# Attention scores from halves of TensorE's rows, joined on three engines

## What is computed

```python
q = apply_rope(q, pos)
k = apply_rope(k, curr_seq_pos + jnp.arange(sk))
scores = jnp.einsum('bhqd,bhkd->bhqk', q, k) / scale
attn = jax.nn.softmax(scores + m[:, None, :, :], axis=-1)
```

## Time and profile before, and how to read it

| | us |
|---|---|
| median of 3 runs | 1569.04 (1567.05 to 1571.4) |
| profiled execution, its own time | 1573.28 |
| its span in the profile | 1571.5 |
| mean granted clock of TensorE | 0.979 of full speed |

### The profile page before, as it was taken

The page is one execution under the profiler, slowest core; times in us unless marked ns, Lnnn a source line. Parts: engine busy times, 40 slices in busy tenths (PEclk is TensorE's granted clock), DMA queues, the critical chain, the costliest instruction groups (busy, mean ns, idle before and its releaser), DMA issues. The chain is left out here.

```text
span 1571.5 us, 26176 instructions
## 1 busy us (share of the span) xinstructions
PE 1491.5 (95%) x8720; PEld 1313.4 (84%) x8720; DVE 1034.3 (66%) x2375; ACT 614.2 (39%) x1183; POOL 722.5 (46%) x586
## 2 busy tenths in 40 slices
PE   6889999999999999999999579999999999949998
PEld 5778888888888888888888479999999999938886
DVE  5737888878888778887788735455455455475552
ACT  5732222322223222222222246555555555455442
POOL 5734445554555545555455334333333333224554
PEclk9989999999999999999999789999999999969999
DMA  7830222212222122221221696343973343152221
GB/s 265 279 108 27 69 74 68 67 53 74 73 67 67 47 80 73 67 67 47 80 67 40 187 345 239 107 127 113 400 274 99 98 127 121 60 207 81 101 74 67
DMA packets 90991, 184.02 MB, mean 117 GB/s; under 512 B 8976, under 2 KB 34064, under 8 KB 90768
## 3 DMA queue, kind: packets, MB, share of 16 engines
q1 hardware_dynamic: 86848, 178.95, 35.5%
q10 hardware_dynamic: 4080, 4.26, 0.8%
HBM read 129.70 MB, written 53.48 MB: 117 GB/s over the span
## 5 line engine op out<-in xcount | busy, mean ns | idle before, releaser
L51 PE MATMUL q_ps<-x_hi,w_hi 128*128 128x512 f32 x1024 | 399.7, 390 | 3.4 <-PEq L66 3.4
L53 PE MATMUL q_ps<-x_hi,w_lo 128*128 128x512 f32 x1024 | 401.2, 392 | 0.0
L52 PE MATMUL q_ps<-x_lo,w_hi 128*128 128x512 f32 x1024 | 400.5, 391 | 0.0
L913 DVE TENSOR_TENSOR vw_lo<-vw_ps,vw_hi 64x256 fp32r<-64x256 f32 x512 | 215.9, 422 | 225.5 <-ACT vw_hi L873 220.4
L902 POOL TENSOR_TENSOR w_lo<-w_raw,w_hi 128x512 fp32r<-128x512 f32 x128 | 166.7, 1303 | 289.0 <-ACT w_hi L865 289.0
L838 PE MATMUL acc_ps<-vw_hi,x_hi 128*128 128x256 f32 x1024 | 290.3, 283 | 1.4 <-ACT vw_hi L873 1.4
L840 PE MATMUL acc_ps<-vw_hi,x_lo 128*128 128x256 f32 x1024 | 290.2, 283 | 0.0
L839 PE MATMUL acc_ps<-vw_lo,x_hi 128*128 128x256 f32 x1024 | 290.2, 283 | 0.0
L873 ACT CAST vw_hi<-vw_ps 64x256 fp32r<-64x256 f32 x512 | 187.5, 366 | 170.3 <-PE vw_ps L53 165.5
L595 POOL TENSOR_TENSOR q_lo<-rot,q_hi 128x512 fp32r<-128x512 f32 x128 | 165.0, 1294 | 190.3 <-ACT q_hi L561 190.2
L51 PEld LDWEIGHTS q_ps<-x_hi,w_hi 128*128 128x128 f32 x1024 | 192.9, 188 | 44.9 <-issue 3.6
(11 more groups left out here) (132 smaller groups left out, 2455.9 us busy)
## 6 DMA issues: line engine op xcount, KB each, us to landing
w_raw<-in_wo SPq DMA_DIRECT2D x128, 256.0 KB, 2.7
w_raw<-in_wq SPq DMA_DIRECT2D x32, 512.0 KB, 5.2
probs_scratch<-pt_hi SPq DMA_DIRECT2D x64, 256.0 KB, 2.6
probs_scratch<-pt_lo SPq DMA_DIRECT2D x64, 256.0 KB, 3.2
x_hi<-probs_scratch SPq DMA_DIRECT2D x32, 512.0 KB, 7.7
x_lo<-probs_scratch SPq DMA_DIRECT2D x32, 512.0 KB, 9.4
x_in<-in_x SPq DMA_DIRECT2D x16, 512.0 KB, 4.8
ahead_y<-in_x SPq DMA_DIRECT2D x8, 1024.0 KB, 6.5
```

The costliest lines, as they stand in the source:

```text
L51: pe.matmul(out, hi, rhs_hi, start=first, stop=False, **kw)
L52: pe.matmul(out, hi, rhs_lo, start=False, stop=False, **kw)
L53: return pe.matmul(out, lo, rhs_hi, start=False, stop=last, **kw)
L913: done = nc.vector.tensor_tensor(vw_lo[at], vw_ps[i][b * SK:(b + 1) * SK, h, :], vw_hi[at].bitcast(F32), ALU.subtract)
```

## The change

`key_hi` and `key_lo` become one tile `key_parts`. In each head's 64 rows it holds the high keys in the head's own 64 columns and the low keys in the other 64. Its zeroing on VectorE goes. The scores of a step are made as products of 64 rows by 128 columns: for each `c`, for `q_hi` and then `q_lo`, one for each head, into a PSUM tile of its own (`st_ps[0]`, `st_ps[1]`). A head's tile then holds its high-key sums in the head's own partitions and its low-key sums in the other 64; the product of low by low is now in the sums, too. ScalarE copies the low sums of both heads into the head's own partitions of `low_scores` (at the head of its slot), GpSimd adds the mask to that tile (at the head of its slot), and VectorE adds the high sums in two operations of 64 partitions, in place of the mask's addition. `rope_ps` goes, to make room in PSUM; the rotation multiplies by the cosine in place in `q_ps`, in another order, and TensorE waits for `rot_ready` before it fills these tiles again.

```diff
--- before.py
+++ after.py
@@ -365,8 +365,7 @@
             return ctx.enter_context(nc.semaphore(name))
 
         key_raw = sb("key_raw", [P, 2, B, SK])
-        key_hi = sb("key_hi", [P, 2, B, P], F32R)
-        key_lo = sb("key_lo", [P, 2, B, P], F32R)
+        key_parts = sb("key_parts", [P, 2, B, P], F32R)
         cos_q = sb("cos_q", [P, S])
         sin_q = sb("sin_q", [P, S])
         mask = sb("mask", [P, B, S])
@@ -374,6 +373,7 @@
         rot = sb("rot", [P, 2, S])
         q_hi = sb("q_hi", [P, 2, S], F32R)
         q_lo = sb("q_lo", [P, 2, S], F32R)
+        low_scores = sb("low_scores", [P, S])
         masked = sb("masked", [P, S])
         shifted = sb("shifted", [P, NBLK, BLK])
         probs = sb("probs", [P, NBLK, BLK])
@@ -386,16 +386,16 @@
         pt_hi = sb("pt_hi", [P, 2, S], F32R)
         pt_lo = sb("pt_lo", [P, 2, S], F32R)
         q_ps = [ps(f"q_ps{i}", [P, S]) for i in range(4)]
-        st_ps = ps("st_ps", [P, S])
+        st_ps = [ps(f"st_ps{h}", [P, S]) for h in range(2)]
         s_ps = ps("s_ps", [P, NBLK, BLK])
-        rope_ps = ps("rope_ps", [P, S])
         part_ps = ps("part_ps", [P, 2, NBLK])
 
         consts_in = sem("att_consts_in")
         w_in = [sem(f"w_in{c}") for c in range(2)]
         w_hi_ready = sem("w_hi_ready")
         w_lo_ready = sem("w_lo_ready")
-        key_zeroed = sem("key_zeroed")
+        st_low_ready = sem("st_low_ready")
+        low_masked_ready = sem("low_masked_ready")
         key_in = sem("key_in")
         key_hi_ready = sem("key_hi_ready")
         key_lo_ready = sem("key_lo_ready")
@@ -418,9 +418,17 @@
 
         block = ctx.enter_context(nc.Block())
 
-        def own_block(part, h):
-
-            return part[h * HALF:(h + 1) * HALF, :, :, h * SK:(h + 1) * SK]
+        def own_rows(h):
+
+            return slice(h * HALF, (h + 1) * HALF)
+
+        def high_keys(h):
+
+            return key_parts[own_rows(h), :, :, h * SK:(h + 1) * SK]
+
+        def low_keys(h):
+
+            return key_parts[own_rows(h), :, :, (1 - h) * SK:(2 - h) * SK]
 
         def raw_keys(h):
 
@@ -504,7 +512,7 @@
                     wait(pe, w_hi_ready, 2 * (hp - 1) + c + 1)
                     wait(pe, w_lo_ready, 2 * (hp - 1) + c + 1)
                 if c == 0 and ks[0] == 0:
-                    wait(pe, prod_ready, 2 * u - 2)
+                    wait(pe, rot_ready, 2 * u - 2)
                 for k in ks:
                     at = (slice(None), k, slice(b * S, (b + 1) * S))
                     last = three(pe, q_ps[2 * (j % 2) + c][:], w_hi[:, c, k, :], w_lo[:, c, k, :], x_hi[at], x_lo[at],
@@ -526,9 +534,12 @@
                     for c in range(2):
                         pe.wait_ge(q_hi_ready, 2 * u - 1 + c)
                         pe.wait_ge(q_lo_ready, 2 * u - 1 + c)
-                        last = three(pe, st_ps[:], key_hi[:, c, b, :], key_lo[:, c, b, :], q_hi[:, c, :], q_lo[:, c, :],
-                                     c == 0, c == 1)
-                    last.then_inc(st_done, 1)
+                        for n, part in enumerate((q_hi, q_lo)):
+                            for h in range(2):
+                                last = pe.matmul(st_ps[h][:], key_parts[own_rows(h), c, b, :], part[own_rows(h), c, :],
+                                                 start=c == 0 and n == 0, stop=c == 1 and n == 1)
+                                if c == 1 and n == 1:
+                                    last.then_inc(st_done, 1)
                 if has(g, j, 0):
                     queries(g, j, 1, range(KT // 2, KT))
 
@@ -545,19 +556,22 @@
             def slot(g, j, last):
                 u = STEPS_G * g + j
                 hp = 2 * g + j // B
+                if has(g, j, 2):
+                    for h in range(2):
+                        act.wait_ge(st_done, 2 * (u - 2) + h + 1)
+                        wait(act, masked_ready, u - 2)
+                        nc.scalar.copy(low_scores[own_rows(h)], st_ps[h][own_rows(1 - h)]).then_inc(st_low_ready, 1)
                 if j % B == 0 and has(g, j, 0) and not (isinstance(g, int) and g == 0 and j == 0):
                     split_w(hp, 1)
                 if j == 1:
                     act.wait_ge(key_in, 64 * (g + 1))
-                    if isinstance(g, int) and g == 0:
-                        act.wait_ge(key_zeroed, 1)
-                    wait(act, st_done, u - 1)
+                    wait(act, st_done, 2 * (u - 1))
                     for h in range(2):
-                        nc.scalar.copy(own_block(key_hi, h), raw_keys(h)).then_inc(key_hi_ready, 1)
+                        nc.scalar.copy(high_keys(h), raw_keys(h)).then_inc(key_hi_ready, 1)
                 if has(g, j, 1):
                     for c in range(2):
                         act.wait_ge(rot_ready, 2 * u - 1 + c)
-                        wait(act, st_done, u - 1)
+                        wait(act, st_done, 2 * (u - 1))
                         nc.scalar.copy(q_hi[:, c], rot[:, c]).then_inc(q_hi_ready, 1)
                 if j % B == B - 1 and not (last and j >= B):
                     split_w(hp + 1, 0)
@@ -581,12 +595,15 @@
             def slot(g, j, last):
                 u = STEPS_G * g + j
                 hp = 2 * g + j // B
+                if has(g, j, 2):
+                    pool.wait_ge(st_low_ready, 2 * (u - 2) + 2)
+                    nc.gpsimd.tensor_tensor(low_scores[:], low_scores[:], mask[:, (j - 2) % B], ALU.add).then_inc(low_masked_ready, 1)
                 if j % B == 0 and has(g, j, 0) and not (isinstance(g, int) and g == 0 and j == 0):
                     split_w(hp, 1)
                 if j == 1:
                     for h in range(2):
                         pool.wait_ge(key_hi_ready, 2 * g + h + 1)
-                        nc.gpsimd.tensor_tensor(own_block(key_lo, h), raw_keys(h), own_block(key_hi, h).bitcast(F32),
+                        nc.gpsimd.tensor_tensor(low_keys(h), raw_keys(h), high_keys(h).bitcast(F32),
                                                 ALU.subtract).then_inc(key_lo_ready, 1)
                         pool.wait_ge(key_lo_ready, 2 * g + h + 1)
                 if has(g, j, 1):
@@ -623,21 +640,22 @@
                 if has(g, j, 1):
                     q1, q2 = q_ps[2 * ((j - 1) % 2)][:], q_ps[2 * ((j - 1) % 2) + 1][:]
                     dve.wait_ge(q_done, 2 * u)
-                    nc.vector.tensor_tensor(rope_ps[:], q1, cos_q[:], ALU.mult)
-                    nc.vector.tensor_tensor(prod[:, 0], q2, sin_q[:], ALU.mult).then_inc(prod_ready, 1)
+                    nc.vector.tensor_tensor(prod[:, 0], q2, sin_q[:], ALU.mult)
                     nc.vector.tensor_tensor(prod[:, 1], q1, sin_q[:], ALU.mult)
+                    nc.vector.tensor_tensor(q1, q1, cos_q[:], ALU.mult).then_inc(prod_ready, 1)
+                    nc.vector.tensor_tensor(q2, q2, cos_q[:], ALU.mult).then_inc(prod_ready, 1)
                     dve.wait_ge(prod_ready, 2 * u - 1)
                     wait(dve, q_lo_ready, 2 * u - 3)
-                    nc.vector.tensor_tensor(rot[:, 0], rope_ps[:], prod[:, 0], ALU.subtract).then_inc(rot_ready, 1)
-                    dve.wait_ge(rot_ready, 2 * u - 1)
-                    nc.vector.tensor_tensor(rope_ps[:], q2, cos_q[:], ALU.mult).then_inc(prod_ready, 1)
+                    nc.vector.tensor_tensor(rot[:, 0], q1, prod[:, 0], ALU.subtract).then_inc(rot_ready, 1)
                     dve.wait_ge(prod_ready, 2 * u)
                     wait(dve, q_lo_ready, 2 * u - 2)
-                    nc.vector.tensor_tensor(rot[:, 1], rope_ps[:], prod[:, 1], ALU.add).then_inc(rot_ready, 1)
+                    nc.vector.tensor_tensor(rot[:, 1], q2, prod[:, 1], ALU.add).then_inc(rot_ready, 1)
                 if has(g, j, 2):
-                    b = (j - 2) % B
-                    dve.wait_ge(st_done, u - 1)
-                    nc.vector.tensor_tensor(masked[:], st_ps[:], mask[:, b], ALU.add).then_inc(masked_ready, 1)
+                    dve.wait_ge(low_masked_ready, u - 1)
+                    for h in range(2):
+                        dve.wait_ge(st_done, 2 * (u - 2) + h + 1)
+                        done = nc.vector.tensor_tensor(masked[own_rows(h)], st_ps[h][own_rows(h)], low_scores[own_rows(h)], ALU.add)
+                    done.then_inc(masked_ready, 1)
                     dve.wait_ge(masked_ready, u - 1)
                     nc.vector.transpose(s_ps[:].rearrange("p n k -> p (n k)"), masked[:]).then_inc(softmax_step, 1)
                     dve.wait_ge(softmax_step, SOFTMAX_STEPS * (u - 2) + 1)
@@ -667,9 +685,6 @@
                     wait(dve, probs_ready, u - 2)
                     nc.vector.reciprocal(row_inv[:], row_sum[:]).then_inc(inv_ready, 1)
 
-            for part in (key_hi, key_lo):
-                done = nc.vector.memset(part[:].bitcast(F32), 0.0)
-            done.then_inc(key_zeroed, 1)
             dve.wait_ge(consts_in, 48)
             over_key_heads(dve, slot, False)
 
```

## The result

The changed kernel takes 1568.11 us (median of 20 runs, 1565.79 to 1571.46), the kernel before, beside it, 1571.61 (20 runs, 1567.05 to 1575.32): a ratio of 0.9983 [0.9975, 0.9991]. The medians differ by 3.5 us, the means by 2.7, which is what the ratio says. A second set of runs gave 0.999 [0.9979, 1.0001], whose interval includes 1. The forecast was +1.0 us. The profiled execution took 1567.43 us, with a span of 1565.6.

What follows compares the result with a forecast made beforehand. TensorE's matmuls were taken to bound the kernel. The profiled 1573.3 us, +3.6 (tail) and -2.6 (steps), gives 1574.3; as the median lies 4.2 below that execution, the forecast was 1570.0 us, range 1543 to 1580.

Steps and rivals of the forecast that it cites:

- Streaming: TensorE's scores: eight half-row matmuls run as four side-by-side pairs of 0.23, 0.92 us instead of 1.38 per step.
- Rival (c): TensorE's scores: the row halves don't run side by side, +0.87 us per step, 1628 us; chance 0.08.
- Changing shape: TensorE around each score block: going to half rows and back costs 0.41 us, plus 0.01 for late second halves.
- 0.04 gained, **2.6 us** over 64 steps: TensorE's scores per step: 1.34 us instead of 1.38, streaming and shape change together.
- (a): TensorE's score block: no price for changing shape, 1543 us, chance 0.14; half the price, 1557 us, chance 0.12.
- (b): TensorE's score block: eight weight loads for six make it slower, 1577 us (chance 0.18) or 1591 us (chance 0.06).
- 1591: Inside the score block a half's next weights wait for its own matmul: 0.33 us per step, 21 us; chance 0.06.
- 1577: The two halves' first weight loads follow one another: 0.11 us more per step, 7 us; chance 0.18.
- VectorE, ScalarE, GpSimd hidden: Attention steps: joins of 0.68 each, copies of 0.60 each and an addition of 1.29 us stay behind TensorE's work.
- The two waits of TensorE: Attention stage of the kernel before: TensorE waits for the others twice, 5.1 and 4.7 us long.
- Tail: End of the attention stage, without cover: the last transposition starts at 898.2 instead of 894.60, 3.6 us later.
- The sum: Whole kernel: +3.6 in the tail less 2.6 in the steps, +1.0 us, the profiled execution at 1574.3.

Runs made afterwards that it cites:

- rotation_alone: The kernel before with only the changed rotation (cosine products in place, new order, TensorE waiting for the rotation's end), scores as before; 1568.64 us, ratio 0.9998.
- tail_early: The changed kernel with the last step's low copies and mask addition issued a slot earlier; 1566.52 us, ratio 0.9978.
- full_shared: Changed kernel with scores over all 128 rows, turning copies and tail work moved earlier, first head's sine product moved from VectorE to GpSimd; 1545.41 us, ratio 0.9849.

## Why the prediction was wrong, point by point

- **Streaming** (side by side, 0.23 per pair): right. The two of a pair start 3 ns apart, and a pair that follows another starts 0.231 behind it. Rival (c) falls.
- **Changing shape** (0.41 + 0.01): the mechanism was right, read off the router's column quarters: 0.32 in, 0.32 out, 0.34 for the second query matmul. The price was 0.39.
- **The step that failed** is the term "0.04 gained, **2.6 us** over 64 steps". The gain measured 0.087 a step, 5.5 us in the stage, so it outweighed the tail's 3.5 and the sum changed its sign. The term is a difference of two large ones, 0.46 saved and 0.42 paid. Of the 0.047 us between forecast and measurement, 0.03 is the price, mis-sized, most of it on the way out. There the prediction took 0.33 - 0.215 = 0.115, with the router's groups, 0.215 apart, as the pitch that was due; the changed kernel shows 0.323 - 0.2315 = 0.09. The 0.215 was no pitch of the columns alone: full matmuls of 256 columns, as many as a router group's, start 0.12 apart in the projection. Another 0.013 was put at nothing: behind the stretch of 1.782 us, the next nine pitches take 2.065 us for 2.078 before, while the 37 further ones take 8.387 in both kernels. Why, no run shows. The rest is rounding.
- **Rivals (a) and (b)**: loads are not made ahead over a change of shape, so (a) falls; inside the block the load for the third pair starts with the second pair (502.60, 502.59), on the same rows, so the 1591 of (b) falls. The halves' first loads run together (`x2`, 502.25, 4 ns apart), so its 1577 falls, too.
- **VectorE, ScalarE, GpSimd hidden**: right. Joins 682 ns for 0.68, copies 581 for 0.60, addition 1297 for 1.29; `rotation_alone` shows the rotation worth nothing to the step. The two waits of TensorE that the prediction read in the earlier trace rows are one, before the last scores, seen once on the loads (5.1) and once on the matmuls (4.7); in the middle of the stage there is none.
- **Tail** (+3.6): right, +3.5; predicted 898.2 - 894.60 from the same chain of `probs`, addition, two joins. `tail_early` took 1.8 of it away.
- **The sum** was +1.0; from the traces it is -2.0. The 3.0 between them is less than the 4.7 us I gave as what can be told, but 20 runs of each kernel told 1.7 parts in a thousand. That the forecast of 1570.0 lies within 1.9 us of the measured 1568.11 is partly luck: it starts from a median of three runs, 2.6 us under that of 20.

## What to carry to other kernels

Halving TensorE's rows gives real concurrency, but going to the half shape and back costs 0.39 us here, so two matmuls saved per visit (0.46) are nearly paid away: batch the visits, or find a layout that keeps all rows, as `full_shared` does. A layout that spares TensorE can shift the bound to the others: look for rings through two engines' program orders, and for VectorE operations with two SBUF inputs beside a busy GpSimd. A new step on a helper engine that is free in the steady state can still cost its latency in a stage's tail: 3.5 us here, half of it for its place in the order.

## What was not expected of the hardware

Row halves ran as two independent lists: four matmuls of one half and then four of the other, in program order, ran as pairs a median of 13 ns apart, at no loss (12.234 us for 12.233 a step). The price of changing shape is nearly the same for two pairs (0.40 us) and for four (0.39). A matmul's pitch is some 0.2315 us in and just behind a block of scores and 0.227 further on. Which of VectorE and GpSimd pays for their meeting depended on which had started: VectorE's two-SBUF product took 0.68 us when it was first and up to 2.74, behind a weight subtraction, when it was second.
